# Feed-forward stage: |h| kept in another buffer, the wait for an older down product put before the GELUs alone, and a tile joined two rounds after its rounding

## What is computed

```python
h = jnp.einsum('bsd,df->bsf', x, w1) + b1      # 512 -> 2048
h = float2fix(h, 8)                            # to multiples of 1/256
h = pwlin_gelu_basic(h, 8, 8)                  # straight lines between GELU's values at steps of 0.25 on [-4, 4]
h = float2fix(h, 8)
out = float2fix(jnp.einsum('bsf,fd->bsd', h, w2) + b2, 8)
```

## The kernel before, in words

| step | engine, line | what | waits for |
|---|---|---|---|
| `round_up(n)` | DVE L2100 | m = product + bias, rounded | up(n) |
| `distance(n)` | ACT L1992, L1994 | a = abs of h, then w = 4 - a in `rest` | round_up(n), and down(n - 4) complete |
| `snap(n)` | DVE L2106, L2108 | v (bf16) = w snapped, then rest = share of the step | distance(n) |
| `ends(n)` | ACT L1999, L2000 | g0, a = GELU at both ends | snap(n) |
| `slope(n)`, `scale(n)` | POOL L1755, L1761 | a = (a - g0), a = a x share | ends(n) |
| `join(n)` | DVE L2114, L2117 | g0 = g0 - 4a, m = max(m, 0) + g0 | scale(n) |
| `high_h(n)` | ACT L2004 | high part of m, into ht | join(n) |
| `low_h(n)` | DVE L2122 | low part of m, into ht | high_h(n) |

## Time and profile before

### The profile page before, as it was taken

How to read it: one execution, slowest core, us unless ns; L and a number is a source line. 1 busy time by engine, 2 the same in 40 slices (tenths; PEclk the granted TensorE clock), 3 DMA queues, 4 the chain that set the end, 5 groups by cost and what they waited for, 6 DMA issues and landing times. The chain is left out here.

```text
span 1613.8 us, 30330 instructions
## 1 busy us (share of the span) xinstructions
PE 1582.4 (98%) x11178; PEld 1383.3 (86%) x11178; DVE 1212.5 (75%) x2387; ACT 1017.3 (63%) x2019; POOL 820.8 (51%) x778
## 2 busy tenths in 40 slices
PE   9999999999999999999999999999999999999997
PEld 7879899998999989899899777989887788787886
DVE  5558888877887888878887783666566778788887
ACT  3357777777877777777776442444435666666675
POOL 3317657475674846746364331333434555555554
PEclk9999999999999999999999999999999999999999
DMA  8974636455463654534443874012116601010010
GB/s 252 288 228 148 181 111 186 123 183 161 134 180 113 189 149 144 180 118 127 131 128 84 266 257 138 14 48 73 60 34 221 236 14 59 21 52 20 8 53 26
DMA packets 191746, 207.19 MB, mean 128 GB/s; under 512 B 82480, under 2 KB 139888, under 8 KB 191600
## 3 DMA queue, kind: packets, MB, share of 16 engines
q1 hardware_dynamic: 191600, 205.27, 41.6%
HBM read 150.68 MB, written 54.53 MB: 127 GB/s over the span
## 5 line engine op out<-in xcount | busy, mean ns | idle before, releaser
L75 PE MATMUL p_bank_score<-p_ctxt,p_qo 128*128 128x256 f32 x2304 | 304.5, 286 | 0.7 <-ACT p_probs L1070 0.3
L75 PEld LDWEIGHTS p_bank_score<-p_ctxt,p_qo 128*128 128x128 f32 x2304 | 288.1, 191 | 5.8 <-issue 2.1
L75 PE MATMUL p_bank_mix<-p_probt,p_ctx 128*128 128x512 f32 x1152 | 292.0, 397 | 0.5
L75 PEld LDWEIGHTS p_bank_mix<-p_probt,p_ctx 128*128 128x128 f32 x1152 | 207.4, 189 | 41.9 <-issue 3.7
L1276 DVE SCALAR_TENSOR_TENSOR p_qo<-p_bank_mix,p_odd,p_qo 128x512 fp32r<-128x512 f32 x192 | 143.8, 749 | 57.6 <-ACT p_qo L1084 50.0
L1084 ACT ACTIVATE p_qo<-p_bank_mix,p_odd 128x512 fp32r<-128x512 f32 x192 | 132.3, 689 | 68.1 <-PE p_bank_mix L75 67.5
L1070 ACT ACTIVATE p_probs<-p_bank_score,p_small 128x257 f32<-128x257 f32 x256 | 121.3, 475 | 59.6 <-DVE p_small L1257 55.6
L764 POOL TENSOR_SCALAR p_probs<-p_probs,p_small 128x256 f32<-128x256 f32 x256 | 121.4, 481 | 70.6 <-DVE p_small L1263 70.5
L758 POOL TENSOR_TENSOR p_ctx<-p_ctx_in,p_ctx 128x768 fp32r<-128x768 f32 x64 | 118.3, 1849 | 66.7 <-ACT p_ctx L1059 66.2
L753 POOL TENSOR_TENSOR p_ctx_in<-p_ctx_in,p_odd_in 128x768 f32<-128x768 f32 x64 | 118.2, 1846 | 42.0 <-DMA p_odd_in<-in_ctx_dram 42.0
L1257 DVE TENSOR_REDUCE p_small<-p_bank_score 128x1 f32<-128x257 f32 x256 | 105.2, 414 | 10.6 <-PE p_bank_score L75 7.9
(11 more groups left out here) (302 smaller groups left out, 3895.6 us busy)
## 6 DMA issues: line engine op xcount, KB each, us to landing
p_blocks_in<-in_ctx_dram SPq DMA_DIRECT2D x256, 96.0 KB, 2.4
p_ctx_in<-in_ctx_dram SPq DMA_DIRECT2D x64, 384.0 KB, 3.2
q<-p_ctx SPq DMA_DIRECT2D x64, 256.0 KB, 3.7
ffn<-p_w_raw SPq DMA_DIRECT2D x64, 256.0 KB, 2.9
p_odd_in<-in_ctx_dram SPq DMA_DIRECT2D x64, 192.0 KB, 3.6
p_x<-in_x_dram SPq DMA_DIRECT2D x32, 256.0 KB, 4.4
p_quad<-q SPq DMA_DIRECT2D x32, 256.0 KB, 3.6
p_probt<-q SPq DMA_DIRECT2D x32, 256.0 KB, 3.8
```

What stands on the lines that cost most here:

```text
L75: made = e.matmul(out, lhsT, rhs, start=n == 0, stop=n == last)
```

## The change

`distance` writes the absolute value into v (bf16) in place of a, so it no longer touches memory of ht; it waits for `scaled` of tile n - 4 (the last reader of the old v) in place of `downed`. The wait for `downed` now stands in `ends`, before the two GELUs, which write g0 and a. DVE's round becomes round_up(n), join(n - 2), snap(n), low_h(n - 2), and ACT's distance(n), high_h(n - 2), ends(n). In the rounds that finish a group the third and fourth output are moved behind snap and low_h on DVE, and the third and fourth `rounded_sum` behind high_h on ACT. No instruction is added or removed, and PE, POOL and SP keep their orders. |h| in bf16 is coarser than 1/256 from 1 on.

```diff
--- before.py
+++ after.py
@@ -1985,17 +1985,19 @@
                              ACT.Copy).then_inc(y_hi, 1)
 
             def distance(n):
-                m, a, w = m_[n % SETS], a_[n % SETS], w_[n % SETS]
+                m, v, w = m_[n % SETS], v_[n % SETS], w_[n % SETS]
                 e.wait_ge(rounded, n + 1)
                 if n >= SETS:
-                    e.wait_ge(downed, NRF * (n - SETS + 1))
-                e.activation(a[:], m[:], ACT.Abs, bias=minus).then_inc(absed, 1)
+                    e.wait_ge(scaled, n - SETS + 1)
+                e.activation(v[:], m[:], ACT.Abs, bias=minus).then_inc(absed, 1)
                 e.wait_ge(absed, n + 1)
-                e.activation(w[:], a[:], ACT.Relu, bias=last, scale=-1.0).then_inc(left, 1)
+                e.activation(w[:], v[:], ACT.Relu, bias=last, scale=-1.0).then_inc(left, 1)
 
             def ends(n):
                 a, g0, v = a_[n % SETS], g0_[n % SETS], v_[n % SETS]
                 e.wait_ge(snapped, n + 1)
+                if n >= SETS:
+                    e.wait_ge(downed, NRF * (n - SETS + 1))
                 e.activation(g0[:], v[:], ACT.Gelu, bias=base).then_inc(gelu0, 1)
                 e.activation(a[:], v[:], ACT.Gelu, bias=quarter).then_inc(gelu1, 1)
 
@@ -2060,12 +2062,18 @@
                 if n == SCALED - 1:
                     after.norm.root(e, 1)
                 for done in done_at(n):
-                    for i in range(NRF):
+                    for i in range(2):
                         rounded_sum(done * NRF + i)
                 if n < NF:
                     distance(n)
+                if 4 <= n < NF + 2:
+                    high_h(n - 2)
+                for done in done_at(n):
+                    for i in range(2, NRF):
+                        rounded_sum(done * NRF + i)
+                if n < NF:
                     ends(n)
-                if n <= NF:
+                if n == 2:
                     high_h(n - 1)
                 for i in tile_at(n, TURNED):
                     after.norm.high(e, i, zts_next[(g + 1) % 2], i % NRF * P)
@@ -2224,25 +2232,30 @@
                 g = n // KF
                 if LAG <= n < NF:
                     round_up(n)
-                if 1 <= n - 2 < NF:
+                if 2 <= n - 2 < NF:
+                    join(n - 2)
+                if n == 3:
                     low_h(n - 2)
-                if n == 3:
                     sums_of(NT - 1)
                     e.wait_ge(y_seen, 2 * NT)
                     after.norm.guard(e, 1)
                 if n == SCALED:
                     after.norm.finish(e, 1)
                 for done in done_at(n):
-                    for i in range(NRF):
+                    for i in range(2):
                         output(done * NRF + i)
-                        if i + 2 < NRF:
-                            down_sum(done * NRF + i + 2)
+                        down_sum(done * NRF + i + 2)
                 if n < NF:
                     for i in tile_at(n, SCALED):
                         scaled_rows(i)
                     snap(n)
-                if n - 1 < NF:
+                if n == 2:
                     join(n - 1)
+                if 2 <= n - 2 < NF:
+                    low_h(n - 2)
+                for done in done_at(n):
+                    for i in range(2, NRF):
+                        output(done * NRF + i)
                 for i in tile_at(n, TURNED):
                     after.norm.low(e, i, zts_next[(g + 1) % 2], i % NRF * P)
                 for done in done_at(n + 1):
```

## The result

The change makes the kernel slower: 1623.53 us (median of 4 runs, 1620.93 to 1625.06) against 1614.15 for the kernel before on the same chip (4 runs, 1613.24 to 1615.0). The ratio is 1.0054, 95% interval 1.0041 to 1.0066. The forecast was 1609.0, its range 1608.0 to 1612.3.

The account below looks back on a forecast made before the run. PE was taken to set the pace, so only its late starts could be won: 2.52 (turns) + 0.45 (double downs) + 2.34 (tail) = 5.31 us off 1614.27 gave 1609.0 us, range 1608.0 to 1612.3.

Parts of the forecast that it names:

- The turns: PE's late starts at turns in the second and third group, waiting for DVE's `low`: all 2.52 us to go.
- The wait for the older down: Moving the wait for down(n - 4) from ACT's distance to the GELUs: cost 0.
- Join and high_h a round later: DVE's join and ACT's high_h: a pair with a turn falls from 11.79 to 10.9 us, a plain round stays 4.94.
- The double downs: Late double downs at the heads of groups: 0.45 of 0.67 us gained by moving two outputs later, bounds 0 and 0.67.
- low_h behind the snap: low_h(n - 2) now ends DVE's round, tightest at down(3) with 0.6 us to spare: cost 0, other end 1 us.
- The tail: down(62) and down(63) wait for DVE's low_h: all 2.34 us to go if DVE has caught up, bounds 0 and 2.34.
- The rule on the lock: Port pair shared by DVE and POOL: the loop snap, GELUs, slope, scale, snap bounds a plain round however the rest is ordered.
- Slower: the snap meets the whole of POOL's scale: Rival: the snap behind the join waits 1.43 us instead of some 0.4, 1.03 more a round; 1619.0 us, chance 0.06.
- Late downs: Rival: late low_h stalls downs at the start or group heads, or half the tail's loss stays; about 1611.6 us, chance 0.14.

Follow-up runs that it names:

- the short instructions: POOL's slope and scale on 64 of the 512 columns: 1608.08 us in the changed kernel, 1609.71 us in the kernel before.
- scale short: The changed kernel with POOL's scale alone on 64 of 512 columns: 1607.33 us, one execution.
- slope short: The changed kernel with POOL's slope alone on 64 of 512 columns: 1608.15 us, one execution.
- low_h last: The kernel before with low_h(n - 2) alone moved to the end of DVE's round, behind join(n - 1): 1675.02 us, ratio 1.0362.

## Why the prediction was wrong, step by step

- **The turns, 2.52 us.** Right in outcome: no turn waits. DVE's idle time before `low` fell from 1.28 to 0.56 us, as forecast, and `low` ends at 1376.10, 2.1 us ahead of the turn that needs it. The pair of rounds is mis-sized: it takes 11.47 us (round_up at 1368.83 and 1380.30), so 0.3 less than 11.79 and not the 0.9 that gave 10.9.
- **The wait for the older down, 0.** Right, and shown by itself: 1614.86 against 1614.66 us.
- **Join and high_h a round later: "A plain round I leave at 4.94".** This is the step that failed. The round takes 5.47 to 5.48. The prediction had read the earlier trace rows as DVE's instructions waiting for POOL's, and had asked only where the snap would fall. It never asked who meets POOL once the snap has moved. Before, the join's second part started just ahead of the slope (the slope's 1.76 is that wait, on POOL's side) and round_up, which reads PSUM, ran beside it. After, the slope starts 0.05 us ahead of the join, so DVE does the waiting, and it does it twice. On top of that high_h stands between the join and the GELUs, which puts the join into the loop. That the new order pays on POOL is shown by the short instructions: the same order runs 15.5 us faster with them, the order before only 4.9.
- **The double downs, 0.45 gained.** Wrong as a consequence. With at most 0.1 us a round to catch up, where some 0.6 had been, the three heads take 6.9 us more and not 0.45 less. The bounds of 0 and 0.67 held no loss, because the term was looked at without the round that feeds it.
- **low_h behind the snap, 0 to 1 us.** Its reckoning took the round of before. In the kernel after low_h itself is quick (0.69), and late because its round is.
- **The tail, 2.34 gained.** Rested on "if DVE has caught up". It has not: the tail is 3.9 us longer and not 2.34 shorter.
- **The rule on the lock.** By the Trainium skill, "SBUF — State Buffer", section "SBUF: two separate sides", whoever of VectorE and GpSimd starts first holds the shared pair for its whole instruction; it names VectorE instructions in a 2-port mode, and those with two SBUF inputs against a GpSimd instruction that reads SBUF. The trace agrees: join 1.79 us when it starts 0.05 behind the slope, 0.69 with the slope at 1.76 when it is the one ahead. The prediction used the rule for the loop through the snap, and didn't go on to the join, which has two SBUF inputs.
- **The rivals.** "Slower: the snap meets the whole of POOL's scale" had the right kind of mechanism at the wrong instruction: the snap fell to 0.28, the join rose. It gave 1619.0 and a chance of 0.06; measured 1623.5. Its switching point, a pair of rounds above 11.59, wasn't reached by the 11.47 measured: the loss came from DVE no longer catching up below that point. (With short POOL instructions PE's own pair in that group takes 11.4 to 11.5 us, so 11.59 was a little high.) Late downs, the first rival, came true in kind too, but with heads and tail 10.8 us longer, where it had priced 2.65 us of gain given up.

## What to carry to other kernels

When two engines take turns on one resource, write out for the new order which of them starts first at each meeting, and cost every instruction that can meet, not only the one that met before. Cost a moved instruction by the loop that it closes, from one start to the same start a round later over all engines, and compare that with the pace of the engine that bounds: slack lost below that pace costs at the next burst of work (5.47 us cost 9 in all), and above it nothing is ever caught up (5.79, 5.98, 6.12 and 6.26 us cost 44, 41, 50 and 59). The plain round alone doesn't rank them: add up a whole period with its turns and outputs. A group of 103.1, 102.1, 105.1 and 107.1 us, against 92.1 before, gives 44, 40, 52 and 60 us for four groups. A part of a reordering tried alone says little about the whole, since each order has another loop.

## What the runs showed of the hardware

- A DVE instruction with two SBUF inputs that starts behind a POOL instruction is recorded as running, not as waiting. It ended 0.54 to 0.56 us behind POOL's recorded end in all the cases read (after, scale short, slope short, low_h last), whether it had started 0.04 or 0.5 us behind it. The busy time of DVE so rises by a wait that no wait view lists.
- It goes both ways: POOL's slope takes 1.29 us by itself or as the first, and 1.75 where a DVE instruction started 0.09 us ahead of it.
- In the tail PE idled 2.18 us, and then its clock fell to the lower level. Windows of the profile after (us, busy of PE, PEld, DVE, ACT, POOL, then PEclk):

```profile
1588.00:1599.00 11.00, 8.82 (x40) 6.81 (x38) 10.86 (x13) 6.84 (x11) 5.45 (x4) 1.00 0.00 0
1599.00:1602.50 3.50, 3.50 (x9) 2.78 (x10) 3.46 (x3) 1.83 (x3) 2.71 (x2) 0.52 0.00 0
```

A granted clock of 0.52 over 3.5 us is about the level of 1.2 GHz; the down in it took 4.57 us where the one before took 2.96. These 1.6 us made nothing later. PE idled 0.88 us behind that down, until DVE's low_h ended (1603.71 + 0.68 = 1604.39, row below), and nothing that feeds this low_h waits for that down. At the full clock PE would have idled 2.5 us, and the next down would have started at the same 1604.45.

```profile
1603.71 0.68 DVE L2130 SCALAR_TENSOR_TENSOR p_ht_q<-p_m,p_ht_q 128x512 fp32r<-128x512 f32 x1
```
